# Graph attention layers re-blocked to 4 target tiles, with masks added by DMA, and a scatter spread over 5 stages

## The chip, the cores and the metric

One core of one Trainium2 chip runs the whole program in one launch. The metric is the device time of an execution in microseconds (us); the kernel before takes a median of 7067.14 us over 3 runs (7049.2 to 7069.41). The engines are TensorE (PE, with its weight loads as PEld), VectorE (DVE), ScalarE (ACT), GpSimd (POOL) and SyncE (SP), which only issues DMAs; 16 DMA engines move the data. Engines run on their own and wait for each other by semaphores.

## The reference

A graph of 3125 nodes with 96 features and 103125 directed edges goes through four blocks, each added to its input and normed: three attention layers (GAT), a GIN layer, dot attention, and a layer with edge features. The change touches the GAT layers most:

```
def _gat_layer(x, src, dst, W, a_src, a_dst, b):
    h = (x @ W).reshape(N, H, C)                       # H = 4 heads, C = 24
    alpha_s = jnp.einsum('nhc,hc->nh', h, a_src)
    alpha_d = jnp.einsum('nhc,hc->nh', h, a_dst)
    e = jax.nn.leaky_relu(alpha_s[src] + alpha_d[dst], NEG_SLOPE)
    m = jax.ops.segment_max(e, dst, num_segments=N)
    ex = jnp.exp(e - m[dst])
    den = jax.ops.segment_sum(ex, dst, num_segments=N)
    alpha = ex / (den[dst] + 1e-16)
    out = jax.ops.segment_sum(h[src] * alpha[:, :, None], dst, num_segments=N)
    return out.reshape(N, H * C) + b
for l in range(W.shape[0]):                            # 3 layers
    x = jax.nn.relu(_gat_layer(x, src, dst, W[l], att_src[l], att_dst[l], bias[l]))
```

The last layer of the network sums `relu(x[src] + edge_attr @ We + be)` over the edges of a target. For it the edges' 32 features are scattered in DRAM into an order by source and target tile; that scatter is independent of everything else until the last layer.

## The kernel before, in words

The graph is held dense: nodes are padded to 3200, 25 tiles of 128. `begin` counts the edges of each pair of nodes into a DRAM table by accumulating indirect DMAs, and `make_tables` (L581) turns the counts into `log_counts`, a 3200 x 3200 float table of log counts with a very low value where there is no edge. Attention over edges is then a dense softmax over source nodes with `log_counts` added to the logits.

`gat_attend` (L751) is one GAT layer. Targets go in 5 blocks of 5 tiles (`BT`, `NB`). For a block j, a chunk c of source tiles (9, 8 and 8) and a head h there is a run, 12 runs to a block, 60 to a layer; a unit is one source tile of a run, 100 units to a block. With s and d the source and target terms, `src_row` holds 0.8 s for all sources in every partition. The steps are:

- `maximum` (L885, VectorE): the largest of `near` (half a row of `log_counts`, loaded by SP) plus `src_row`, for a target tile, a head and a half; 40 to a block. The maxima of the next block are spread over the runs of the present one. `columns` (L896) makes the per-target bias `dst_bias` of them.
- `add_bias` (L971, ScalarE): `logit = mask + dst_bias`, where `mask` is a piece of `log_counts` in SBUF, loaded once for four heads. In the last block three of five tiles have it on VectorE instead (L906).
- `finish_logit` (L916, VectorE): `logit = max(src_row, least) + logit`, for each target tile and run, one run ahead of its use; `logit` has 2 buffers.
- TensorE turns each unit's 5 tiles of 128 x 128 into `psE` (L1042, 2 buffers), ScalarE takes the exp of 640 columns into `prob` (L1000), with 0.2 s as its per-source bias, and TensorE multiplies it with the values `hx` (L1029). The values of two source tiles run at once in two groups of 32 columns of the array; heads take the others. A unit's values follow its transposes by `LAG` = 3 units.
- At a block's end ScalarE copies `psO` out, TensorE turns it back, and VectorE sums two parts, divides by the denominator and adds the bias (`output`, L927, 7 chained steps).

The order on every engine is the order in the text of its block; each engine waits at the instruction whose semaphore is not there yet, and all that is queued behind it waits too. SP's loads are sorted by the unit at which their buffer comes free. GpSimd does nothing in a layer but `edge_scatter` (L692), which takes the edges in 62 groups of 13 columns, a third of them in each layer (`LAYER_GROUPS`); each group is two loads, two copies and 13 indirect DMAs of 128 rows of 136 bytes, in 3 stage buffers. `dot_attend` and `make_tables` leave GpSimd idle.

## Time and profile before

| What | us |
|---|---|
| Median of 3 runs | 7067.14 |
| Lowest and highest | 7049.2, 7069.41 |
| The profiled execution | 7061.88 |
| Its span in the trace | 7060.0 |
| Table of logs (`make_tables`) | about 1756 to 1996 |
| First GAT layer, then a projection | about 2003 to 2869, to 2909 |
| Dot attention | about 4960 to 5560 |

Times in the trace count from the start of the span. A group of instructions has a line, an engine, an operation, its output and inputs, their shapes, a count, a busy time and a mean. "Idle before" is the time that the engine stood before them, and behind the arrow is what ended it. PEclk is the clock that TensorE was granted, as a share of 2.4 GHz. Matmuls overlap, and records of VectorE and ScalarE overlap a little, so the cost of one in a row of several is read from start to start. A float32 matmul is two instructions. In the table of stretches a row is start:end, the length, then busy us and instructions of PE, PEld, DVE, ACT and POOL, the granted clock, the busy share of the 16 DMA engines and GB/s.

### The profile page before, as it was taken

Reading aid. Unit: us, or ns where it says so; the run is one execution under the profiler, and the core shown is the slowest. Engines: PE = TensorE matmul, PEld = TensorE weight load, DVE = VectorE, ACT = ScalarE, POOL = GpSimd, SP = SyncE. Lnnn points to the kernel's source line nnn. Section 1 sums busy time; section 2 is a strip of 40 time slices with the busy share of each in tenths; the row PEclk is TensorE's granted clock in tenths of the full one; section 3 lists DMA queues with packets and bytes.
Section 4 is the critical chain, followed back from the end, with each engine's and each line's share of the span. In section 5 each row is a group of like instructions: output and inputs, shape, how many; then the busy total and the mean of one; then the engine's idle time right before and its main releaser. Section 6 shows DMA issues by size and latency. Waiting matters only on the chain. (4 is left out here: it accounts for less than half of the span.)

```text
span 7060.0 us, 64068 instructions
## 1 busy us (share of the span) xinstructions
PE 3859.8 (55%) x22802; PEld 2278.1 (32%) x22802; DVE 4197.0 (59%) x4408; ACT 2725.0 (39%) x3720; POOL 3458.3 (49%) x2713
## 2 busy tenths in 40 slices
PE   2111111110528889488895788877888555445544
PEld 1111011110524445244453444544333233223332
DVE  1434443332789998699986999965899612112113
ACT  1000000000428888288883788840666311111111
POOL 0888878887058830488402884000000155555552
PEclk6555555555769999799997899988888656666566
DMA  9222222222953432233322333233212111111112
GB/s 314 12 7 18 21 15 7 0 0 14 342 203 116 131 108 73 89 112 119 115 78 84 120 117 106 95 121 125 84 66 75 33 39 42 42 39 40 42 40 25
DMA packets 363334, 570.34 MB, mean 81 GB/s; under 512 B 168173, under 2 KB 246027, under 8 KB 358926
## 3 DMA queue, kind: packets, MB, share of 16 engines
q1 hardware_dynamic: 185086, 495.29, 20.9%
q0 software_dynamic: 174720, 69.73, 9.6%
q8 instruction: 187, 3.06, 0.2%
q10 hardware_dynamic: 3216, 1.23, 0.1%
q14 instruction: 125, 1.02, 0.0%
HBM read 451.64 MB, written 114.40 MB: 80 GB/s over the span
## 5 line engine op out<-in xcount | busy, mean ns | idle before, releaser
L313 POOL DMA_INDIRECT counts<-plcell_add,plcell_slot x806 | 1308.8, 1624 | 439.8 <-issue 236.0
L1522 POOL DMA_INDIRECT emxg<-xtab,emsrc x832 | 803.5, 966 | 571.0 <-DVE emsrc L1564 313.5
L396 DVE TENSOR_REDUCE plnlow<-plsame 128x13 f32<-128x1664 bf16 x62 | 117.0, 1888 | 1039.4 <-DMA counts<-plcell_add,plcell_slot 1039.4
L329 PE MATMUL plrows<-ident,plcell 128*128 128x128 f32 x806 | 185.9, 421 | 952.3 <-DVE plsame L388 951.7
L644 ACT ACT_TABLE_LOAD x1 | 1.3, 1283 | 1713.8 <-PE mtps L632 1713.8
L1607 PE MATMUL emps_m<-emwe,emfeatT 128*128 128x384 f32 x416 | 280.0, 768 | 680.5 <-ACT emfeatT L1546 360.6
L1513 POOL IOTA emlocal_id<- 128x128 f32 x1 | 0.2, 237 | 1260.0 <-POOLq L1052 1260.0
L1574 DVE TENSOR_TENSOR emsame<-emlocal_id,emrow 128x512 f32<-128x512 f32 x208 | 144.4, 694 | 695.5 <-DMA plbase_row<-slot_base 488.1
L1546 ACT ACTIVATE emfeatT<-emps_f 128x128 f32<-128x128 f32 x208 | 57.6, 277 | 1198.6 <-remote 746.3
L329 PEld LDWEIGHTS plrows<-ident,plcell 128*128 128x128 f32 x806 | 161.4, 224 | 985.4 <-DVE plsame L388 984.6
L1042 PE MATMUL ga0psE<-ident,ga0logit 128*128 128x128 f32 x2500 | 354.7, 286 | 196.6 <-DVE ga0logit L925 172.3
L1042 PE MATMUL ga2psE<-ident,ga2logit 128*128 128x128 f32 x2500 | 358.0, 287 | 182.8 <-DVE ga2logit L925 165.7
L1042 PE MATMUL ga1psE<-ident,ga1logit 128*128 128x128 f32 x2500 | 354.4, 286 | 187.1 <-DVE ga1logit L925 164.3
L743 POOL DMA_INDIRECT sorted_edges<-ga0sstage,ga0sslot x273 | 385.8, 1413 | 82.8 <-issue 76.8
L1000 ACT ACTIVATE ga2prob<-ga2psE,ga2src_fifth 128x640 f32<-128x640 f32 x500 | 378.5, 793 | 106.6 <-PE ga2psE L1042 101.3
L1000 ACT ACTIVATE ga1prob<-ga1psE,ga1src_fifth 128x640 f32<-128x640 f32 x500 | 377.9, 793 | 105.0 <-PE ga1psE L1042 102.2
L1000 ACT ACTIVATE ga0prob<-ga0psE,ga0src_fifth 128x640 f32<-128x640 f32 x500 | 378.3, 792 | 103.3 <-PE ga0psE L1042 96.7
L743 POOL DMA_INDIRECT sorted_edges<-ga1sstage,ga1sslot x273 | 376.4, 1379 | 82.8 <-issue 76.8
L925 DVE SCALAR_TENSOR_TENSOR ga2logit<-src_row,ga2least,ga2logit 128x1024 f32<-128x1024 f32 (+1 forms) x300 | 396.1, 1341 | 34.1 <-ACT ga2logit L980 31.3
L925 DVE SCALAR_TENSOR_TENSOR ga1logit<-src_row,ga1least,ga1logit 128x1024 f32<-128x1024 f32 (+1 forms) x300 | 396.6, 1343 | 33.1 <-ACT ga1logit L980 32.0
L925 DVE SCALAR_TENSOR_TENSOR ga0logit<-src_row,ga0least,ga0logit 128x1024 f32<-128x1024 f32 (+1 forms) x300 | 397.7, 1346 | 31.2 <-ACT ga0logit L980 28.0
L1616 PEld LDWEIGHTS emps_a<-emmsg,emsame 128*128 128x128 f32 x1664 | 338.2, 272 | 196.7 <-issue 196.1
(320 smaller groups left out, 9525.9 us busy)
## 6 DMA issues: line engine op xcount, KB each, us to landing
counts<-plzeros SPq DMA_DIRECT2D x32, 1250.0 KB
mthalf<-counts SPq DMA_DIRECT2D x50, 800.0 KB, 10.1
log_counts<-mtlogs SPq DMA_DIRECT2D x25, 1600.0 KB
ga0near<-log_counts SPq DMA_DIRECT2D x50, 800.0 KB
ga1near<-log_counts SPq DMA_DIRECT2D x50, 800.0 KB
ga2near<-log_counts SPq DMA_DIRECT2D x50, 800.0 KB
ginhalf<-counts SPq DMA_DIRECT2D x50, 800.0 KB, 7.3
dotlogs<-log_counts SPq DMA_DIRECT2D x25, 1600.0 KB, 6.7
```

The source lines that it names most:

```text
L313: nc.gpsimd.indirect_dma_start(counts[t % 2][:, :], bass.IndirectOffsetOnAxis(ap=cell_slot[:, g % 2, j:j + 1], axis=0), cell_add[:, g % 2, ...
L329: last = nc.tensor.transpose(rows[:, j * P:(j + 1) * P], cell[:, g * G + j:g * G + j + 1].to_broadcast([P, P]), ident[:])
L396: step(nc.vector.reduce_sum(nlow[:], same[:], axis=AX.X))
L743: nc.gpsimd.indirect_dma_start(edges["sorted"][:, :], bass.IndirectOffsetOnAxis(ap=slot[:, t:t + 1], axis=0), stage[:, k, t - i * G, :], N ...
L925: nc.vector.scalar_tensor_tensor(part, src_row[:, h, first:first + width], least[:, j * BT + q, h:h + 1], part, ALU.max, ALU.add).then_inc ...
L1000: nc.scalar.activation(prob[:, u % P_BUFS, :], psE[:, u % 2, 0:BW], ACT.Exp, bias=src_fifth[:, tile(r, t), h:h + 1]).then_inc(exp_ready, 1)
L1042: last = nc.tensor.transpose(psE[:, u % 2, q * P:(q + 1) * P], logit[:, r % 2, q, t * P:(t + 1) * P], ident[:])
L1522: nc.gpsimd.indirect_dma_start(xg[:, h, t, :], None, xtab[:, :], bass.IndirectOffsetOnAxis(ap=src[:, h, t:t + 1], axis=0)).then_inc(gather ...
L1546: nc.scalar.activation(featT[:, v % 2, :], ps_f[:, 0:P], ACT.Copy).then_inc(feat_kept, 1)
L1574: nc.vector.tensor_tensor(same[:, v % 2, :, :], local_id[:].unsqueeze(1).to_broadcast([P, CT, P]), row[:, g % ROWS, lo:lo + CT, ED:ED + 1] ...
L1607: nc.tensor.matmul(ps_m[:, v % 2, 0:CT * D], featT[:, v % 2, :], we[:].rearrange("p t d -> p (t d)"), start=True, stop=True).then_inc(pre_ ...
L1616: last = nc.tensor.matmul(flat_a[:, bass.ds(lo, D)], same[:, w % 2, t, :], msg[:, w % 2, t, :], start=False, stop=(w == CHUNKS - 1 and t = ...
```

## The change

In `gat_attend` the blocks become six of 4 tiles and one of 1 tile (84 runs). Tiles 2 and 3 of a block of four (12 of the 25) are no longer biased by ScalarE and finished by VectorE: VectorE's new `clamp` writes `max(src_row + dst_bias, low_bias)` into `logit`, with `low_bias = dst_bias + least`, and GpSimd issues a DMA that adds `log_counts` to it in SBUF, once per head, with no `mask` buffer. The other 13 tiles keep both steps, and their masks have 4 buffers. Logits are made 2 runs ahead in 3 buffers. The exp takes 512 columns (128 in the last block), `psE` has 3 buffers and `prob` 8. The values of 4 source tiles run at once in the 4 column groups of the array, for one head at a time, and go with the last of their 4 units; the four parts are summed when they are turned back, by small matmuls with `fold` (four identities of 32 on top of each other), so that `output` has 5 steps. Each head's `psO` is kept by ScalarE behind its last run, and `turn_output` follows in run 1 of the next block. The maxima of the next block end in run 9 and its columns stand behind them. The scatter is a generator: GpSimd issues the adds of run r+2, then its share of scatters. Its 62 groups are split 3 to `make_tables`, 16 to each layer and 11 to `dot_attend`, and it has 2 stage buffers.

```diff
-LAYER_GROUPS = ((0, 21), (21, 42), (42, 62))
+TABLE_GROUPS = (0, 3)
+LAYER_GROUPS = ((3, 19), (19, 35), (35, 51))
+DOT_GROUPS = (51, 62)
@@ edge_scatter
-    STAGES = 3
+    STAGES = 2
+                yield t
@@ gat_attend
+        BLOCK_TILES = (4, 4, 4, 4, 4, 4, 1)
-        P_BUFS = 5
-        M_BUFS = 6
+        FOUR = P // VW
+        ADDED = (2, 3)
+        BIAS_AT = (1, 5)
+        P_BUFS = 8
+        M_BUFS = 4
+        E_BUFS = 3
+        AHEAD = 2
+        L_BUFS = AHEAD + 1
+        MAX_RUNS = RUNS - AHEAD
+        steps_done = lambda r: scatter_steps * (r + 1) // len(runs)
@@ GpSimd
-                scatter(pool)
+                def add_masks(r):
+                    for i, q in enumerate(added_tiles(j)):
+                        row = (block_first[j] + q) * P
+                        pool.wait_ge(clamped, add_count[r] + i + 1)
+                        pool.dma_start(logit[:, r % L_BUFS, q, 0:width], log_counts[row:row + P, first:first + width], accum_op=ALU.add).then_inc(mask_added[r % L_BUFS], 16)
+                for r in range(len(runs)):
+                    if r + AHEAD < len(runs):
+                        add_masks(r + AHEAD)
+                    while done < steps_done(r):
+                        next(scattering)
+                        done += 1
@@ VectorE
+                def clamp(r, q):
+                    if r >= L_BUFS:
+                        dve.wait_ge(turned, run_end(r - L_BUFS))
+                    nc.vector.tensor_scalar(logit[:, r % L_BUFS, q, 0:width], src_row[:, h, first:first + width], dst_bias[:, j % 2, q, h:h + 1],
+                                            low_bias[:, j % 2, q, h:h + 1], ALU.add, ALU.max).then_inc(clamped, 1)
+                    if ahead is not None:
+                        for q in added_tiles(ahead):
+                            clamp(r + AHEAD, q)
+                    if run == MAX_RUNS - 1 and j + 1 < BLOCKS:
+                        columns(j + 1)
@@ ScalarE
+                        for at, q in zip(BIAS_AT, kept_tiles(runs[r + AHEAD][0])):
+                            if t == at:
+                                add_bias(r + AHEAD, q)
@@ TensorE
-                    if t % 2 == 0 and t + 1 < RUN_TILES[c]:
+                    if t % FOUR != FOUR - 1 and t + 1 < RUN_TILES[c]:
                         return
+                    for w in range(v - t % FOUR, v + 1):
+                        s = units[w][1]
+                        row = (s % FOUR) * VW
+                        last = nc.tensor.matmul(psO[row:row + VW, h, 0:width], hx[:, tile(r, s), h, :], prob[:, w % P_BUFS, 0:width],
+                            wait(pe, mask_added[r % L_BUFS], 16 * adds_in_buffer(r))
+                    for q in range(BLOCK_TILES[j]):
+                        for h in range(HEADS):
+                            last = nc.tensor.matmul(psT[:, q, h, :], o_sb[:, h, q * P:(q + 1) * P], fold[:], start=True, stop=True)
@@ make_tables and dot_attend
+        scatter, _ = edge_scatter(nc, ctx, a, edges, "mts", *TABLE_GROUPS)
+        scatter, _ = edge_scatter(nc, ctx, a, edges, "dots", *DOT_GROUPS)
```

## Rows read from the trace of the kernel before

**Rows 1.** The page: span, and busy time of each engine.

```profile
span 7060.0 us, 64068 instructions
...
PE 3859.8 (55%) x22802; PEld 2278.1 (32%) x22802; DVE 4197.0 (59%) x4408; ACT 2725.0 (39%) x3720; POOL 3458.3 (49%) x2713
```

**Rows 2.** The table of stretches (columns as told above).

```profile
1756.00:1996.00 240.00, 123.54 (x625) 116.05 (x625) 172.50 (x51) 97.33 (x126) 0.00 (x0) 0.69 0.96 335
...
2003.00:2088.00 85.00, 0.00 (x0) 0.00 (x0) 75.48 (x87) 0.83 (x1) 69.28 (x52) 0.50 0.53 173
...
2088.00:2239.00 151.00, 122.97 (x816) 71.30 (x817) 149.69 (x143) 131.42 (x153) 127.33 (x103) 0.92 0.36 118
...
2239.00:2394.00 155.00, 130.87 (x880) 73.89 (x879) 149.00 (x147) 132.38 (x156) 131.35 (x103) 0.96 0.36 116
...
2544.00:2694.00 150.00, 126.48 (x853) 71.02 (x851) 141.35 (x145) 129.46 (x154) 7.42 (x6) 0.97 0.32 111
...
2694.00:2869.00 175.00, 161.89 (x1152) 93.42 (x1152) 131.86 (x141) 128.66 (x162) 0.00 (x0) 0.99 0.14 45
...
4960.00:5560.00 600.00, 494.56 (x3961) 203.21 (x3962) 562.89 (x522) 399.85 (x624) 0.00 (x0) 0.85 0.19 64
```

**Rows 3.** Groups by form, 2090 to 2700 (busy us, mean ns).

```profile
L925 DVE SCALAR_TENSOR_TENSOR ga0logit<-src_row,ga0least,ga0logit 128x1024 f32<-128x1024 f32 x152 | 196.5, 1310 | 4.7 <-ACT ga0logit L980 4.0 <-issue 0.5
...
L980 ACT ACTIVATE ga0logit<-ga0mask,ga0dst_bias 128x1024 f32<-128x1024 f32 x153 | 175.2, 1145 | 14.2 <-DMA ga0mask<-log_counts 12.5 <-PE ga0psE L1042 1.7
...
L925 DVE SCALAR_TENSOR_TENSOR ga0logit<-src_row,ga0least,ga0logit 128x1152 f32<-128x1152 f32 x80 | 113.8, 1438 | 14.4 <-ACT ga0logit L980 11.9 <-issue 2.5
...
L980 ACT ACTIVATE ga0logit<-ga0mask,ga0dst_bias 128x1152 f32<-128x1152 f32 x78 | 97.8, 1258 | 3.0 <-DVE ga0col L903 1.8 <-DVE ga0dst_bias L904 1.2
```

**Rows 4.** VectorE in order of time, block 0 (start us, us, line, operation).

```profile
2139.11 1.27 DVE L925 SCALAR_TENSOR_TENSOR ga0logit<-src_row,ga0least,ga0logit 128x1024 f32<-128x1024 f32 x1
...
2140.31 1.86 DVE L893 CUSTOM_DVE_ANT_0 ga0unused<-ga0near,src_row 128x1600 bf16<-128x1600 f32 x1
...
2142.10 1.27 DVE L925 SCALAR_TENSOR_TENSOR ga0logit<-src_row,ga0least,ga0logit 128x1024 f32<-128x1024 f32 x1
```

**Rows 5.** All engines in order of time, last block of the layer.

```profile
2789.28 1.14 ACT L980 ACTIVATE ga0logit<-ga0mask,ga0dst_bias 128x1024 f32<-128x1024 f32 x1
...
2790.22 0.77 PE L1042 MATMUL ga0psE<-ident,ga0logit 128*128 128x128 f32 x5
...
2790.31 0.78 ACT L1000 ACTIVATE ga0prob<-ga0psE,ga0src_fifth 128x640 f32<-128x640 f32 x1
...
2793.51 0.75 DVE L914 TENSOR_SCALAR ga0logit<-ga0mask,ga0dst_bias 128x1024 f32<-128x1024 f32 x1
...
2793.85 1.48 ACT L1000 ACTIVATE ga0prob<-ga0psE,ga0src_fifth 128x640 f32<-128x640 f32 x2 [0.35 <-PE ga0psE L1042]
...
2794.17 3.67 DVE L925 SCALAR_TENSOR_TENSOR ga0logit<-src_row,ga0least,ga0logit 128x1024 f32<-128x1024 f32 x3
...
2794.29 1.27 PE L1029 MATMUL ga0psO<-ga0prob,hx 128*32 128x320 f32 x8
...
2795.49 1.31 PE L1042 MATMUL ga0psE<-ident,ga0logit 128*128 128x128 f32 x10
...
2796.73 1.27 PE L1029 MATMUL ga0psO<-ga0prob,hx 128*32 128x320 f32 x8
```

**Rows 6.** TensorE in order of time, dot attention: values in four column groups.

```profile
5209.40 1.28 PE L1376 MATMUL dotpsO<-dotwork,hx 128*32 128x320 f32 x16
```

**Rows 7.** ScalarE's groups of the whole span: a 128-column activation from PSUM.

```profile
L1546 ACT ACTIVATE emfeatT<-emps_f 128x128 f32<-128x128 f32 x208 | 57.6, 277 | 1198.6 <-remote 746.3 <-PE emps_f L1603 330.1 <-issue 122.2
```

**Rows 8.** GpSimd's issue of a direct DMA (min/median/max ns, first and last start).

```profile
L724 POOL DMA_DIRECT2D ga0sfeat<-in_edge_attr_dram x21: 541/590/596, 2006.0 to 2475.4; - x21
```

**Rows 9.** GpSimd's scatters, 2390 to 2540, grouped.

```profile
L743 POOL DMA_INDIRECT sorted_edges<-ga0sstage,ga0sslot x80 | 109.2, 1365 | 24.2 <-issue 22.6 <-POOL ga0sstage L740 1.7
```

**Rows 10.** Finishing steps, 2560 to 2690, where GpSimd is idle.

```profile
L925 DVE SCALAR_TENSOR_TENSOR ga0logit<-src_row,ga0least,ga0logit 128x1024 f32<-128x1024 f32 x27 | 34.2, 1279 | 1.3 <-ACT ga0logit L980 1.3
```

More of the change, by code:

```diff
@@ L600, in make_tables, with _ @@
         pieces = [(j, k) for j in range(NB) for k in range(NB)]
+        scatter, _ = edge_scatter(nc, ctx, a, edges, "mts", *TABLE_GROUPS)
         with nc.Block() as block:
+            @block.gpsimd
+            def _(pool):
+                for _ in scatter(pool):
+                    pass
             @block.sync
@@ L706, in edge_scatter, with steps @@
     scattered = [sem(f"scattered{k}") for k in range(STAGES)]
-    def run(pool):
+    def steps(pool):
         pool.dma_start(slot[:], edges["slot"][:, first * G:last * G]).then_inc(tables_loaded, 16)
@@ L772, in gat_attend @@
         sem = lambda n: nc.alloc_semaphore(tag + n)
+        BLOCK_TILES = (4, 4, 4, 4, 4, 4, 1)
+        BLOCKS = len(BLOCK_TILES)
+        block_first = [sum(BLOCK_TILES[:j]) for j in range(BLOCKS)]
+        MOST = max(BLOCK_TILES)
+        DW = MOST * P
         RUN_TILES = (9, 8, 8)
@@ new lines, in gat_attend @@
+                    g = block_first[j] + q
+                    free = (g - 1) * MAX_PER + HEADS * f + HEADS if g else 0
+                    before = max_run[free - 1] if g else -1
+                    when = first_unit[before] if before >= 0 else -1 + (8 * g + 4 * f) / 100
+                    loads.append((when, 0, ("near", g, f, free)))
+        for n, (j, c, q) in enumerate(mask_uses):
+            if n < M_BUFS:
+                loads.append((-1 + (n + 9) / 100, 1, ("mask", j, c, q, 0)))
+            else:
+                oj, oc, oq = mask_uses[n - M_BUFS]
+                r = oj * RUNS + oc * HEADS + HEADS - 1
+                i = kept_tiles(oj).index(oq)
+                loads.append((first_unit[max(r - AHEAD, 0)] + BIAS_AT[i], 1, ("mask", j, c, q, act_count[r] + i + 1)))
@@ L904, in columns @@
[L904 to L914 removed]
+                    nt = BLOCK_TILES[j]
@@ L927, in output @@
+                    part = logit[:, r % L_BUFS, q, 0:width]
+                    nc.vector.scalar_tensor_tensor(part, src_row[:, h, first:first + width], least[:, block_first[j] + q, h:h + 1], part, ALU.max, ALU.add).then_inc(logit_ready, 1)
                 def output(j):
+                    nt = BLOCK_TILES[j]
                     dve.wait_ge(o_turned, j + 1)
                     step = Chain(dve, out_steps, j * OUT)
-                    yb = y[:, j * BT:(j + 1) * BT, :]
-                    for e in range(2):
-                        for k in range(2):
-                            part = psO[:, k, :, :].rearrange("p f c -> p (f c)")[:, 0:BW].rearrange("p (q h e c) -> p q h e c", h=2, e=2, c=VW)[:, :, :, e, 0:VC]
-                            total = o_sum[:, :, 2 * k:2 * k + 2, :]
-                            last = nc.vector.tensor_tensor(total, total, part, ALU.add) if e else nc.vector.tensor_copy(total, part)
-                        step(last)
@@ new lines, in output @@
+                    step(nc.vector.tensor_scalar(rden[:, 0:nt, :], psT[:, 0:nt, :, DH], 1e-16, None, ALU.add))
+                    step(nc.vector.reciprocal(rden[:, 0:nt, :], rden[:, 0:nt, :]))
+                    step(nc.vector.tensor_tensor(yb.rearrange("p q (h c) -> p q h c", h=HEADS), psT[:, 0:nt, :, 0:DH],
+                                                 rden[:, 0:nt, :].unsqueeze(3).to_broadcast([P, nt, HEADS, DH]), ALU.mult))
+                    step(nc.vector.tensor_tensor(yb, yb, bias[:].unsqueeze(1).to_broadcast([P, nt, D]), ALU.add))
@@ L942, in output @@
                     step(nc.vector.tensor_scalar(yb, yb, 0.0, None, ALU.max))
                     assert step.n == OUT
-                for n in range(MAXIMA):
-                    maximum(0, n)
+                for n in range(max_end(0)):
+                    maximum(n)
                 columns(0)
-                for q in range(BT):
-                    finish_logit(0, q)
+                for r in range(AHEAD):
+                    for q in added_tiles(0):
+                        clamp(r, q)
+                    for q in kept_tiles(0):
+                        finish_logit(r, q)
@@ L962, in _ @@
                             output(j - 1)
-                    if run == RUNS - 2 and j + 1 < NB:
+                    assert next_max == until
+                    if run == MAX_RUNS - 1 and j + 1 < BLOCKS:
                         columns(j + 1)
-                output(NB - 1)
+                output(BLOCKS - 1)
             @block.scalar
@@ L1340, in dot_attend, with _ @@
         flat = lambda n: psS[:, n % S_BUFS, :, :].rearrange("p a c -> p (a c)")[:, 0:BW]
+        scatter, _ = edge_scatter(nc, ctx, a, edges, "dots", *DOT_GROUPS)
         with nc.Block() as block:
+            @block.gpsimd
+            def _(pool):
+                for _ in scatter(pool):
+                    pass
             @block.sync
```

261 lines of the change are left out of this document (123 added, 138 removed).

## The prediction

> **What bounds the kernel now.** I read the page first [rows 1]: no engine is busy over 60% of the span, so the bound is found by stage. The table of stretches of the first attention layer gives it [rows 2]. The layer lasts from 2003 to 2869, 866 us, and the three layers are alike. For 85 us only VectorE works: the 40 maxima of the first block. Then come four stretches of 150 to 155 us, a block of 5 target tiles each (three have rows), with VectorE 141 to 150 us busy, TensorE 123 to 131, ScalarE 129 to 132: VectorE sets the pace. The last 175 us have no maxima; there TensorE is the fullest (162) and the run period is set by it. The projection that follows is unchanged. GpSimd's scatters end before 2544, long before the layer does. The chain of waits covers only the last norm and says nothing here, so the argument goes by stretches, forms and spacing. In the forms [rows 3] and the order of time [rows 4] I take starts, not durations, because VectorE's records overlap: a finishing step of 1024 columns costs 1.20 us (2139.11 to 2140.31), a maximum with its read 1.79 (to 2142.10). The 1152 form is 0.13 longer [rows 3], so a finishing step is 1.24 on average over chunks of 9, 8 and 8 tiles. Check: 60 x 1.24 + 40 x 1.79 = 146, and some 5 for output and columns, 151 against the 150 to 155 of the blocks.
>
> **The change part by part, one layer.**
> *Masking.* 12 of 25 target tiles take a clamp (tensor_scalar on src_row) and an accumulating DMA in place of ScalarE's bias and VectorE's finishing step. 144 tile-runs change. The nearest row of the clamp is the L914 tensor_scalar, 0.75 long and 0.66 before its successor [rows 5]; with the wider form 0.68. VectorE gives back 144 x (1.24 - 0.68) = 81 us, and 36 bias steps of the last block, 25 us.
> *Period of a run in the 4-tile blocks.* An iteration with maxima holds 2 clamps, 2 finishing steps and 3.2 maxima: 1.37 + 2.49 + 5.73 = 9.6 us. For ScalarE, one exp of a pair of 640 columns costs 0.69 (1.48 less 0.78) and at the slope of its 1024 and 1152 forms 0.11 less for 512 [rows 3]: 0.59; a bias 1.03 (2789.28 to 2790.31) to 1.14 [rows 5]. With 8.33 units, and two biases at 1.07: 4.9 + 2.1 = 7.0. For TensorE, two units now take 2.44 (2794.29 to 2796.73) [rows 5]: transposes at 0.108 (5 in 0.77, 10 in 1.31), so 1.08 for ten, some 1.07 of values (the record's 1.27 less a last 0.2 of depth) and 0.3 between. Values of 4 column groups at once are shown by the dot layer: 16 instructions (2 halves, 4 groups, two passes) of 320 columns in 1.28 us [rows 6], as long as the 8 of 2 groups [rows 5]. So a group of 4 tiles of 512 columns costs 1.07 / 2 x 512 / 320 = 0.85 and 0.3 between: 8.33 x 4 x 0.108 + 2.33 x 1.15 = 6.3. Where VectorE has slack, then, ScalarE paces at 7.0; the last stretch, where TensorE paces, still has it busy only 162 of 175 us [rows 2], so for the coupling I put a tenth on top: 7.8. If the 4 groups ran as two pairs, TensorE would need 8.3.
> *A new stall.* All maxima of the next block now end in run 9 of 12, and its columns behind them. The bias of the next block's first run stands in ScalarE's queue at unit 1 of run 10, ahead of run 10's remaining exps, and VectorE reaches the columns only when it has prepared run 11. So ScalarE and behind it TensorE stand for about one iteration, and then VectorE, whose runs 10 and 11 hold only 3.9 us each, waits for two runs at the pace of ScalarE: 15 us in place of 8. A block is 10 x 9.6 + 15 + 3.5 (output, columns) = 114 us; five are 571.
> *Ends.* First maxima: 32 in place of 40 at 1.9, so 85 becomes 69 to the columns, and 9 for preparing two runs instead of one. Block 5, with 8 maxima only, goes by ScalarE: 12 x 7.8 = 94. Block 6 is one tile in 100 units: an exp of 128 columns lasts 0.28 [rows 7], and with one bias a run 3.4 to 4: 43 us, a cost that five equal blocks didn't have. Its tail is 4. Sum 69 + 9 + 571 + 94 + 43 + 4 = 790 against 866: 76 less a layer, 228 for three.
> *The accumulating DMA.* GpSimd issues two a run. No row shows one of this size. Issue: a direct DMA of 127 rows takes 0.59 [rows 8], an indirect one 1.37 [rows 9]; two are 1.2 to 2.7 us a run. A run also issues 2.5 scatters, at 1.9 us each with their copies (80 in 150 us) [rows 9]: 4.7. GpSimd has 6 to 7.4 us of work in 9.6 and is covered. Landing: TensorE wants run r+2 some 6 us after its clamps at the earliest, and because buffers go round in three, a landing up to some 18 us late delays nobody. Traffic: the engines move 335 GB/s at share 0.96 and 111 at 0.32 [rows 2], 348 when full. Per run the near halves (8 of 0.82 MB a block) take 1.6 us, kept masks 0.8, scatters 0.2 (the share is 0.04 higher with some 80 of them in 150 us, 0.08 us each), and the two added tiles 3.1 if an accumulated byte costs as much as a copied one. That is 5.7 of 9.6; at twice the price 8.8, just under. I take it as hidden. Its floor is the copy (no gain below it), its ceiling is open and is the rival below. The Trainium skill, Collectives: The Full Stack, section "The bandwidth ceiling", puts the price of an add in a DMA at its two source reads, half the rate of a copy; by it the sum stays as it is. No row here shows it.
> *Against the change.* The records show GpSimd and VectorE in each other's way: a finishing step lasts 1.31 us over the blocks that are mostly with scatters, 1.28 in a stretch without [rows 3, 10]. The clamp meets the same queue, and its DMAs are issued from it. The Trainium skill, SBUF — State Buffer, box on "DVE blocks DMA", says that such a two-port step keeps GpSimd from writing descriptors; by it landing is late by at most a step's 0.7 us, which the three buffers cover, and the sum would not move.
> *Scatter in 5 stages.* A layer keeps 16 groups of 21. GpSimd passes its last add at about run 69 and then has 37 scatters, 70 us at 1.9, beside 3 runs, the last block and the tail, also 70: even, so 0, at worst 10 a layer. 39 scatters go into the table stage, whose DMA share is 0.96 [rows 2]; 1.4 MB at 335 GB/s are 4 us, with small writes up to 20; I take 5. 143 go into the dot layer, where VectorE is busy 563 of 600 us. The blocks with scatters are 2 us longer on average than the one without for some 80 of them [rows 2]: 4, up to 30 as its tensor_scalar has two ports' worth of reads. Together 9. Output folded by small matmuls into one accumulation is within the stated ends.
> *Sum.* Against the profiled execution, 7061.9 us (span 7060.0): 7062 - 228 + 9 = 6843; its time lies 5 below the median of 7067, so 6848, told as 6850.
>
> **The rivals.**
> *A. The accumulating DMA is the bound (slower).* With added bytes at k times the copy, a run needs 2.6 + 3.1k us of the DMA engines; from k = 2.25 that passes 9.6. At k = 3 a run is 12.0: 60 runs lose 144 and the 12 of block 5 some 40, 184 a layer, so 6850 + 552 = 7400. It loses to the present kernel from about k = 2.5, 1.1 us more a run. For it: the stage of counting accumulates in DRAM and only 2 bytes a row. Against it: a rule of two reads. Between k = 2.25 and 2.5 it eats part of the gain.
> *B. Coupling stays loose (faster, less).* Waits among clamp, DMA, bias and exp bring the 72 four-tile runs to 10.6 us and the last block to 60: 60 x 1.0 + 12 x 2.8 + 17 = 111 a layer, less the boundary waits already in the sum (35), is 76: the gain is gone, 7078. Half of this is likelier, 6965. For it: in the last stretch no engine is full, TensorE at 162 of 175 [rows 2]. Against it: three buffers where there were two.
> *C. No stall at the columns (faster, more).* If ScalarE's queue gets past the bias, the two runs cost 8 and not 15: 5 x 7 x 3 = 105 less, 6745.
> *D. The clock.* TensorE is granted 0.92 to 0.98 while busy 123 to 131 of 150 [rows 2]. In block 6 it works under half the time. At the level of 1.2 GHz a one-tile run still needs less than 5 us; it costs 0 to 10 a layer and stays in the range.
>
> **How the numbers follow.** Forecast with its bounds (6790 to 6910) 0.46; C and what lies near it 0.12; B at half its price, or A just beyond its threshold 0.20; B in full, about equal 0.05; A in full 0.17. The range takes the first three and part of the others: 6740 to 7060. A measurement tells a change from none at about 0.3%, 21 us. Faster: 0.46 + 0.12 + 0.20 = 0.78. Same 0.05. Slower 0.17.
>
> **What would show it.** The clamp's group at 0.75 to 0.85 us, 144 a layer; finishing steps down to 156; blocks of 114 us with a VectorE idle of some 7 us, released by ScalarE, before the first finishing step of each; exps of 512 near 0.68; a last block near 43 us; DMA share near 0.8 to 0.9 at 200 GB/s in the blocks, and TensorE never waiting long for a DMA on the logit tiles. If TensorE's waits before the transposes go to the DMA and the share is over 0.95, A is true. If GpSimd ends each layer alone, the scatter tail is it. Wrong would also be a table stage longer by over 20 us or a dot layer by over 30.

## The result, and the profile after

The changed kernel takes 6994 us (median of four, 6974 to 7006) against 7067 for the kernel before: ratio 0.990, interval 0.9875 to 0.9925, 73 us less. The forecast was 6850, 217 less. The time lies in the range, but two thirds of the forecast gain are missing. The profiled execution took 6973.75 us, 88 less than that of before; it is the fastest of the four, 20 below the median, so the traces show 88 of a forecast 219.

The page of the changed kernel, to be read beside [rows 1] (PEclk, DMA and GB/s are the span in 40 slices):

```profile
span 6972.0 us, 62328 instructions
...
PE 3698.9 (53%) x21452; PEld 2183.6 (31%) x21452; DVE 3889.8 (56%) x4318; ACT 2472.8 (35%) x4050; POOL 4020.6 (58%) x3151
...
DMA  9222222222979987398962898752222111111111
...
q0 software_dynamic: 237024, 305.69, 28.3%
```

VectorE has 307 us less to do, ScalarE 252 less, TensorE 161 less, and the span is only 88 shorter. The first question is therefore not what the work cost but where VectorE now stands idle. One stretch from the start of the first layer to the norm behind the third answers it, in both kernels (columns: stretch and its length, busy time and instructions of PE, PEld, DVE, ACT, POOL, then granted clock, DMA share, GB/s). Before:

```profile
2003.20:4697.00 2693.80, 2081.68 (x13912) 1186.57 (x13912) 2392.05 (x2492) 1990.52 (x2394) 1343.75 (x1060) 0.91 0.31 103
```

After:

```profile
2001.00:4598.10 2597.10, 1913.65 (x12562) 1090.16 (x12562) 2079.47 (x2402) 1737.39 (x2724) 1513.13 (x1257) 0.83 0.75 172
```

VectorE's work in the three layers falls by 313 us (104 a layer); the stretch falls by 97 (32 a layer). Its idle time grows from 302 to 518 us. That is where the gain went: of the 216 us more, 41 lie in the blocks before the last of full size and 175 behind that block's columns, where the three layers end; none lie at the front. The other stages did what was forecast: the table stage went from 246.6 to 251.5 us (+5, as told), the dot layer from 634.5 to 642.0 (+7.5, told +4), the last stage +1, the GIN layer +2; some 7 us less at the very start are not of this change.

The first layer by its own stretches, the counterpart of [rows 2], counted from the columns of one block to those of the next: to the first columns; block 0; block 3; block 5 (the last of four tiles); and, from its first run on, block 6 (one tile).

```profile
2001.00:2068.70 67.70, 0.00 (x0) 0.00 (x0) 59.79 (x71) 0.00 (x0) 0.00 (x0) 0.50 0.43 143
2068.70:2180.60 111.90, 80.16 (x520) 45.77 (x520) 105.95 (x117) 77.90 (x111) 75.15 (x61) 0.84 0.92 209
2414.50:2530.80 116.30, 92.48 (x632) 53.55 (x632) 108.95 (x123) 87.17 (x128) 78.72 (x61) 0.90 0.90 206
2646.60:2740.80 94.20, 88.18 (x618) 50.68 (x619) 66.89 (x75) 86.35 (x128) 71.47 (x65) 0.96 0.93 194
2758.80:2825.10 66.30, 56.24 (x341) 29.17 (x337) 14.96 (x16) 40.21 (x114) 27.92 (x27) 0.53 0.03 7
```

The reader is to see three kinds of stretch. In the middle ones VectorE is nearly full (109 of 116.3). At the front (67.7 us) it works alone, and nothing else can. At the end, in blocks 5 and 6, it has 67 and 15 us of work in 94 and 66, and in the 18 us between the two stretches hardly any. An end of one tile costs 66 us here, 77.9 and 75.1 in the other two layers, and VectorE sleeps through it.

Groups by form in the second layer, to be read beside [rows 3]:

```profile
L928 DVE CUSTOM_DVE_ANT_0 ga1unused<-ga1near,src_row 128x1600 bf16<-128x1600 f32 x200 | 366.2, 1831 | 8.9 <-DMA ga1near<-log_counts 6.7
L958 DVE SCALAR_TENSOR_TENSOR ga1logit<-src_row,ga1least,ga1logit 128x1024 f32<-128x1024 f32 x104 | 136.2, 1310 | 62.0 <-ACT ga1logit L1017 43.6 <-issue 18.4
L898 POOL DMA_DIRECT2D ga1logit<-log_counts x144 | 136.1, 1065 | 292.1 <-DVE ga1logit L949 287.0 <-issue 5.0
L958 DVE SCALAR_TENSOR_TENSOR ga1logit<-src_row,ga1least,ga1logit 128x1152 f32<-128x1152 f32 x52 | 73.9, 1425 | 66.5 <-ACT ga1logit L1017 57.8 <-issue 8.7
L949 DVE TENSOR_SCALAR ga1logit<-src_row,ga1dst_bias,ga1low_bias 128x1024 f32<-128x1024 f32 x96 | 73.8, 809 | 0.1
L949 DVE TENSOR_SCALAR ga1logit<-src_row,ga1dst_bias,ga1low_bias 128x1152 f32<-128x1152 f32 x48 | 40.2, 879 | 2.2 <-PE ga1psE L1086 2.0
```

Finishing steps and maxima last what they lasted. The clamp, 144 a layer, takes 0.81 and 0.88 us; the accumulating DMA 1.07 us of GpSimd's time to issue. Of VectorE's idle time before finishing steps, 128 us in this layer, 101 end with ScalarE's bias, L1017.

The waits in block 3 of the first layer:

```profile
PE ga0psE L1086 <- DMA ga0logit<-log_counts: 11.6, 5, 5.0
...
ACT ga0logit L1017 <- DVE ga0low_bias L941: 7.1, 1, 7.1
...
DVE ga0logit L958 <- ACT ga0logit L1017: 6.3, 4, 2.5
```

### The profile page after: what moved, and what is told of

Same layout as the page of the kernel before. It is cut to its first block and busy times, and to the rows that moved or that the text cites. A ratio compares the mean times of both kernels' runs of the same rounds, so it can differ in the third digit from the quotient of the medians.

```text
span 6972.0 us, 62328 instructions
## 1 busy us (share of the span) xinstructions
PE 3698.9 (53%) x21452; PEld 2183.6 (31%) x21452; DVE 3889.8 (56%) x4318; ACT 2472.8 (35%) x4050; POOL 4020.6 (58%) x3151
## 3 DMA queue, kind: packets, MB, share of 16 engines
q0 software_dynamic: 237024, 305.69, 28.3%
q14 instruction: 131, 1.07, 0.0%
## 5 line engine op out<-in xcount | busy, mean ns | idle before, releaser
L1086 PE MATMUL ga0psE<-ident,ga0logit 128*128 128x128 f32 x2500 | 406.9, 303 | 219.1 <-DMA ga0logit<-log_counts 151.4
L1040 ACT ACTIVATE ga1prob<-ga1psE,ga1src_fifth 128x512 f32<-128x512 f32 (+1 forms) x700 | 405.4, 667 | 153.6 <-PE ga1psE L1086 130.5
L1040 ACT ACTIVATE ga2prob<-ga2psE,ga2src_fifth 128x512 f32<-128x512 f32 (+1 forms) x700 | 405.0, 665 | 152.0 <-PE ga2psE L1086 123.6
L1040 ACT ACTIVATE ga0prob<-ga0psE,ga0src_fifth 128x512 f32<-128x512 f32 (+1 forms) x700 | 405.6, 669 | 139.4 <-PE ga0psE L1086 124.9
L1086 PEld LDWEIGHTS ga2psE<-ident,ga2logit 128*128 128x128 f32 x2500 | 293.7, 151 | 448.1 <-issue 265.1
L1086 PEld LDWEIGHTS ga0psE<-ident,ga0logit 128*128 128x128 f32 x2500 | 293.8, 151 | 447.0 <-issue 252.9
L1086 PEld LDWEIGHTS ga1psE<-ident,ga1logit 128*128 128x128 f32 x2500 | 291.3, 150 | 453.0 <-issue 280.2
L1668 PE MATMUL emps_a<-emmsg,emsame 128*128 128x96 f32 x1664 | 387.5, 375 | 22.8 <-DVE emsame L1626 8.5
L1470 ACT ACTIVATE dotwork<-dotpsS 128x640 f32<-128x640 f32 x500 | 313.1, 708 | 205.9 <-PE dotpsS L1418 204.5
L1502 DVE TENSOR_TENSOR dotwork<-dotwork,dotcnt 128x1280 f32<-128x1280 f32 x250 | 374.8, 1499 | 8.6
```

The source lines that it names most:

```text
L1040: nc.scalar.activation(prob[:, u % P_BUFS, 0:width], psE[:, u % E_BUFS, 0:width], ACT.Exp, bias=src_fifth[:, tile(r, t), h:h + 1]).then_in ...
L1086: last = nc.tensor.transpose(psE[:, u % E_BUFS, q * P:(q + 1) * P], logit[:, r % L_BUFS, q, t * P:(t + 1) * P], ident[:])
L1470: nc.scalar.activation(work[:, t % W_BUFS, 2 * g:2 * g + 2, f * HW:(f + 1) * HW], psS[:, n % S_BUFS, :, 0:HW], ACT.Exp).then_inc(exp_ready, 1)
L1502: nc.vector.tensor_tensor(w, w, cnt[:, t % C_BUFS, cols].unsqueeze(1).to_broadcast([P, HEADS, HW]), ALU.mult).then_inc(prob_ready, 1)
L1668: last = nc.tensor.matmul(flat_a[:, bass.ds(lo, D)], same[:, w % 2, t, :], msg[:, w % 2, t, :], start=False, stop=(w == CHUNKS - 1 and t = ...
```

## The experiments

Every run is compared with the kernel before on the same chip (medians 7050 and 7063 there, and 6726 for the two runs that are marked). For the layers I give beside the time the length of the stretch shown above, first near load of layer 0 to the norm behind layer 2, from each profiled execution (before 2693.8, changed kernel 2597.1), because it leaves out what other stages do from run to run: on the first two of these chips they took, from that norm to the end, 2351 to 2402 us, though no edit here touches them. A stretch is one execution.

**Scatters done before the last block.**

```diff
-        steps_done = lambda r: scatter_steps * (r + 1) // len(runs)
+        steps_done = lambda r: scatter_steps * min(r + 1, 6 * RUNS) // (6 * RUNS)
```

> The same scatters, spread over the runs of the first six blocks (2.9 a run in place of 2.5), so that GpSimd is done before the one-tile block. Theory G (in the changed kernel the last block takes 66 to 78 us because TensorE and ScalarE stand while GpSimd issues its last scatters; once GpSimd is done, a run takes 4.0 us): the block falls to 12 x 4.0 and some 6 for the fold of block 5, 54 us, so 12 to 24 less a layer, 50 for three: 6940. Theory S (the gaps come from the short runs themselves, the chain bias, finish, transpose, exp): the block keeps 66 to 78 us and the time stays at 6990 within 15.

Measured: 6932 us, ratio 0.982 (0.979 to 0.984); stretch 2560.0. The one-tile block takes 57.3, 57.2 and 56.9 us in the three layers where it took 66.3, 77.9 and 75.1, 48 less in all. The stretch is only 37 shorter, because the blocks of four in layer 2 became 10 us longer together. In the second layer of the changed kernel, the stretch of that block up to shortly after GpSimd's last scatter, and the stretch behind it:

```profile
3628.30:3662.70 34.40, 16.69 (x96) 9.70 (x88) 5.93 (x8) 8.54 (x23) 25.23 (x27) 0.55 0.06 13
3662.70:3706.20 43.50, 41.00 (x249) 19.67 (x249) 8.99 (x7) 31.56 (x91) 0.00 (x0) 0.50 0.00 1
```

and the whole block in this kernel, where GpSimd is silent:

```profile
3613.20:3670.40 57.20, 55.25 (x341) 28.82 (x337) 14.93 (x15) 39.72 (x114) 0.00 (x0) 0.54 0.00 1
```

With GpSimd issuing, 23 instructions of ScalarE are done in 34 us; without, 91 in 43. The changed kernel in order of time shows how (start, length, engine; in brackets the idle time before):

```profile
3651.53 0.48 PE L1086 MATMUL ga1psE<-ident,ga1logit 128*128 128x128 f32 x1
...
3651.92 0.37 ACT L1040 ACTIVATE ga1prob<-ga1psE,ga1src_fifth 128x128 f32<-128x128 f32 x1
...
3652.50 0.69 PE L1086 MATMUL ga1psE<-ident,ga1logit 128*128 128x128 f32 x2
...
3659.85 0.96 POOL L750 DMA_INDIRECT sorted_edges<-ga1sstage,ga1sslot  x1 [0.30 <-issue]
...
3662.76 0.37 ACT L1040 ACTIVATE ga1prob<-ga1psE,ga1src_fifth 128x128 f32<-128x128 f32 x1 [10.46 <-remote]
3663.18 0.18 PEld L1086 LDWEIGHTS ga1psE<-ident,ga1logit 128*128 128x128 f32 x1 [10.39 <-ACT ga1prob L1040]
3663.18 0.48 PE L1086 MATMUL ga1psE<-ident,ga1logit 128*128 128x128 f32 x1 [9.99 <-ACT ga1prob L1040]
```

ScalarE stands for 10.46 us, and the view names no instruction that released it ("remote"). TensorE stands behind it, and both go on 2 us after the last scatter is issued.

The semaphore events in the same trace say what ScalarE lacked. Its next exp waits for `turned`, which TensorE raises with each transpose. The transpose of that exp starts at 3651.53, and the next rise of `turned` is recorded at 3662.74, 11.2 us later; the exp starts 0.02 us behind it. In the edited kernel, with GpSimd silent, the rise comes 0.49 us after the start of the transpose. I summed these late rises, where ScalarE stood for one: they cost 9.3, 20.7 and 18.9 us in the one-tile blocks of the changed kernel, some 4 us in each block 5, and nothing in the blocks before it. In the edited kernel they cost nothing in the one-tile blocks, which are 8.9, 20.7 and 18.2 us shorter. So the whole standstill is TensorE's signal that comes late. Whether the transpose itself is held up or only its signal, and by what of GpSimd's scatters (their issue or their writes), the records do not tell: the ends of matmuls are modelled.

Theory G holds: the block falls to 57, and S, which kept 66 to 78, falls. Against the forecast of 43 + 4, some 10 us a layer are left even so.

**The added tiles copied instead of accumulated.**

```diff
-... log_counts[row:row + P, first:first + width], accum_op=ALU.add).then_inc(...)
+... log_counts[row:row + P, first:first + width]).then_inc(...)
```

> The 144 DMAs a layer onto logit copy and don't accumulate: the same bytes from the same queue, and what is left out is the clamped term of target tiles 2 and 3 of each block, so their attention is not the layer's. Theory D (the accumulating DMAs, twice as dear per packet in the records, hold the four-tile blocks at 116.5 us in place of the 114 forecast): blocks fall to 112 or less, 15 to 25 less a layer, about 6930. Rival (VectorE sets the pace, the DMA is hidden in the three buffers): the DMA share falls from over 0.9 to near 0.65, the blocks stay within 1 us and the time within 15 us of 6990.

Measured: 6953 us, ratio 0.986 (0.984 to 0.988); stretch 2576.3. The same block and its bytes:

```profile
2402.20:2518.50 116.30, 93.73 (x632) 54.36 (x632) 108.24 (x123) 87.17 (x128) 73.25 (x61) 0.90 0.60 206
```

The block is as long as before, 116.3 us at the same 206 GB/s, while the share falls from 0.90 to 0.60. The four middle blocks of the three layers average 117 us in both kernels. TensorE's waits before the transposes that end with a landing are 11.6 us in this block of the changed kernel and 6.7 with the copy, and the 5 us less shorten nothing. So the accumulation costs the DMA engines 0.30 x 116.3 = 35 us a block, and costs the block nothing: D is wrong, the DMA is hidden. The 35 us are for 24 DMAs of 0.55 MB on average, 1.45 us each; at the 348 GB/s of [rows 2] a copy of that size takes 1.57, so an accumulated byte costs 1.9 times a copied one (an estimate from these rows). The line of the queue on the two pages agrees, for the same bytes 28.3% with accumulation and here

```profile
q0 software_dynamic: 237024, 305.69, 19.0%
```

which is about 1.5 us more for each of the 432 DMAs. The Trainium skill (Collectives: The Full Stack, section "The bandwidth ceiling") says that an add in a DMA needs two source reads where a copy needs one; it tells this of ReduceScatter. The 1.9 here agrees with it.

The stretch is 21 us shorter all the same. Block 0 went from 112, 111 and 115 us to 106 in the three layers, which is 20 of the 21. The first transposes start 10.2 us behind the columns with the accumulating DMA and 7 to 8 with the copy, so about 3 of the 6 us are the first landing; the rest is not separated. The last block varies as in the changed kernel (76.6, 67.5, 76.4).

**Three tiles of four accumulated.**

```diff
-        ADDED = (2, 3)
-        BIAS_AT = (1, 5)
+        ADDED = (1, 2, 3)
+        BIAS_AT = (1,)
```

> From the changed kernel: three tiles of each block masked by accumulating DMA. By work, VectorE has 12 x 0.6 less a block (101 us). The DMA engines are busy 105 us of 116.5 with two; the plain copy of the same bytes had them busy 70 of 117, so 24 accumulating DMAs cost 70 and 36 cost 105, with 25 to 30 of other traffic: 130 to 135 us. Theory A (beyond a share near 1 the DMA sets the block): blocks of 133, block 5 near 115, a layer longer by 5 x 16.5 + 20 = 103, so 6990 + 310 = 7300. If the DMA never set the pace: blocks of 110 and 6890.

Measured: 7035 us, ratio 0.996 (0.994 to 0.998); stretch 2663.6. A block in the middle:

```profile
2419.50:2539.50 120.00, 98.74 (x648) 57.81 (x645) 103.89 (x123) 76.96 (x117) 87.09 (x73) 0.87 1.06 245
```

VectorE has 5 us less to do than with two added tiles, ScalarE 10, and the block is not shorter: 114 to 120 us. The recorded share is 1.06, the highest of any run; it adds up the times of packets, so it can pass 1. TensorE waits seven times for more than 1.5 us in this block, 19 us in all, and by the records of landings each of these waits ends 0.1 us after an added tile lands. From the last issue of a run's added tiles to their landing it takes 14.9 us (median), where it took 9.3 with two tiles and 5.1 with two plain copies. So rival A of the prediction is real and lies one tile further on. The engines' time, 1.06 x 120 = 127 us, is near the 130 told; wrong was to take 1 for the highest share that the record can show, so blocks are 114 to 120 and not 133.

**One tile of four accumulated.**

```diff
-        ADDED = (2, 3)
-        BIAS_AT = (1, 5)
+        ADDED = (3,)
+        BIAS_AT = (1, 4, 6)
```

> Only tile 3 of each block is masked by DMA, tile 2 goes back to ScalarE's bias and VectorE's finishing step. If VectorE and ScalarE set the pace (rival of D): a run with maxima is longer by a finishing step less a clamp, 1.30 - 0.75 = 0.55, so 50 x 0.55 = 28 a layer and block 5 longer by 12 biases of 1.1, 13: three layers +120, 7110. Theory D (the accumulating DMAs hold the blocks): half their traffic gone gives back 3 us a run before VectorE's 0.55 is paid; the blocks stay at 116 or fall, and the time is 6990 or less.

Measured: 7139 us, ratio 1.012 (1.008 to 1.016), slower than before; stretch 2763.4. Blocks are 129.3 us in place of the 122 forecast:

```profile
2438.50:2567.80 129.30, 98.42 (x632) 56.38 (x632) 114.31 (x122) 99.72 (x140) 61.26 (x49) 0.88 0.61 147
```

and the wait that grew in it:

```profile
DVE ga0logit L958 <- ACT ga0logit L1017: 14.6, 7, 6.0
```

VectorE's work grew by 5.4 us, as told; the other 8 are VectorE waiting for biases, 14.6 us a block where it was 6.3, because ScalarE now has three biases a run. A second cause is mixed in: three kept tiles share the 4 mask buffers that two had, and ScalarE waits 27 us in the first layer for masks to be loaded, for which it does not wait in any other kernel with added tiles. A tile masked by DMA is worth more than its VectorE time in this kernel; how much of that is the mask buffers was not tested. With one tile of four the kernel loses against the one before.

**The one-tile block first.**

```diff
-        BLOCK_TILES = (4, 4, 4, 4, 4, 4, 1)
+        BLOCK_TILES = (1, 4, 4, 4, 4, 4, 4)
```

> The one-tile block comes first. Theory S or G alike (the one-tile block is dear because it stands at the end, where VectorE has no maxima left, and the first maxima stand alone): 8 first maxima in place of 32, 15 us and not 68; a one-tile block beside the 32 maxima of the next takes 32 x 1.85 + 12 x 1.35 and the columns, some 80; five blocks of 116.5; the last of four tiles 94; 9 to prepare and 4 to end: 785 a layer against 827 to 839. So 6990 - 3 x 48 = 6845. If instead the boundary waits or the near loads eat it (a short first block has its 32 maxima behind loads that start late), the gain is under half, 6920 or more.

Measured: 6860 us, ratio 0.973 (0.971 to 0.974); stretch 2486.1. The first layer: first maxima, the one-tile block beside 32 maxima, a full block, the last:

```profile
2002.00:2018.40 16.40, 0.00 (x0) 0.00 (x0) 15.57 (x21) 0.00 (x0) 11.87 (x8) 0.50 0.60 213
2018.40:2095.30 76.90, 43.64 (x256) 20.15 (x256) 74.07 (x81) 39.73 (x99) 35.31 (x24) 0.50 0.36 116
2326.80:2443.40 116.60, 92.15 (x632) 53.31 (x632) 108.99 (x124) 86.86 (x128) 79.09 (x61) 0.90 0.90 206
2690.00:2790.70 100.70, 95.40 (x673) 55.07 (x672) 44.35 (x46) 84.43 (x128) 57.73 (x57) 0.97 0.71 133
```

The same instructions, 62328 of them, in another order: the short block lies where VectorE is busy anyway (74 of 77 us), and the exposed maxima fall from 68 to 16 us. Forecast 6845; a gain of some 120 us over the changed kernel by the ratios, 111 by the stretch, where 144 were told.

**Columns one run earlier.**

```diff
-        MAX_RUNS = RUNS - AHEAD
+        MAX_RUNS = RUNS - AHEAD - 1
```

> From the changed kernel: the maxima of the next block end in run 8 and its columns follow there, one run earlier. Theory C (the wait of ScalarE for the columns, 9.4 us at each boundary, costs VectorE the 6 to 7 us that it stands idle per block): 5 x 6.5 = 33 less a layer, 6990 - 98 = 6892. Rival R (VectorE has only moved its slack: nine runs now hold 3.56 maxima and last 10.4 us, 94; three runs hold none and go by ScalarE's 7.2 to 7.8, 23): a block stays at 117 to 120 and the time at 6990 to 7030, though the wait for the columns is gone from the records.

Measured: 7001 us, ratio 0.991 (0.989 to 0.994); stretch 2639.3, 42 us longer than in the changed kernel, with blocks of 119 to 123 behind the first. In such a block:

```profile
DVE ga0logit L958 <- ACT ga0logit L1017: 9.7, 4, 4.6
```

The wait of ScalarE for the columns, 7.1 us in the changed kernel, is gone from the list, and nothing is won: VectorE now idles 9.7 us for biases. Rival R holds; C, as this edit realizes it, falls. Nine crowded runs and three empty ones cost VectorE more than the wait did. The edit moves the maxima together with the columns, so it takes the run with the columns left where they were, below, to part the two.

**Maxima in every run.**

```diff
-        max_until = lambda j, run: max_first(j) + BLOCK_TILES[j] * MAX_PER * min(run + 1, MAX_RUNS) // MAX_RUNS
...
+        max_points = [(0, max_end(0))] + [(j * RUNS + MAX_RUNS, max_end(j + 1)) for j in range(BLOCKS - 1)]
+
+        def max_until(r):
+            for (t0, n0), (t1, n1) in zip(max_points, max_points[1:]):
+                if r + 1 <= t1:
+                    return n0 + (n1 - n0) * (r + 1 - t0) // (t1 - t0)
+            return max_points[-1][1]
```

This stands on top of the two edits before it (one-tile block first, columns one run earlier). The dots stand for a table, `max_run`, that follows the new order.

> One-tile block first; columns one run earlier; and the maxima no longer stop for the boundary: in the three runs behind the columns VectorE already takes the first maxima of the block after the next, so that each run holds 2.67 of them. If VectorE sets the pace (busy 109 of 116.5 us in a block): a block falls to 110 or 111, six less in six blocks of three layers, 108: 6860 - 108 = 6752. Rival D (the DMA engines, busy 0.90 of 116.5 us = 105, are the next limit): their share passes 0.95, transposes wait for landings, and blocks stay at 114 or more: 6815 and up.

Measured: 6769 us, ratio 0.9585 (0.955 to 0.962); stretch 2396.0. A block and the three layers:

```profile
2419.00:2527.00 108.00, 91.65 (x628) 53.59 (x620) 107.65 (x122) 86.06 (x128) 79.95 (x62) 0.92 0.96 222
...
1995.90:4391.90 2396.00, 1905.29 (x12562) 1094.80 (x12562) 2077.29 (x2403) 1738.46 (x2724) 1592.74 (x1257) 0.86 0.81 187
```

VectorE is busy 107.65 of 108.00 us: it has no wait left in the middle blocks, and the DMA engines are at 0.96 beside it without being the limit. VectorE's work in the stretch is what it was in the changed kernel (2077 against 2079); its idle time fell from 518 to 319 us, and that is the whole gain of 201. This kernel beats both.

**The same, with the columns left where they were.** This run and the next were on another chip, on which the kernel before takes 6726 us, because the last stage is quicker there; ratios are compared, not times.

```diff
-        MAX_RUNS = RUNS - AHEAD - 1
+        MAX_RUNS = RUNS - AHEAD
```

> As the kernel with maxima in every run (6769), but the columns stay behind run 9 of 12, as in the changed kernel. If the maxima behind the columns do all the work and the place of the columns none: VectorE is busy to the end of the block anyway, 6770 within 15. If ScalarE's wait for the columns (7 to 9 us at a boundary) still comes back to VectorE through the biases of the next block's first run: some 3 to 6 us in six blocks of three layers, 6820 to 6870.

Measured: 6443 us, ratio 0.958 (0.957 to 0.960), against 0.9585 with the columns earlier; stretch 2399.8 against 2396.0. In a middle block (108.4 us) ScalarE still waits 7.3 us for the columns, as in the changed kernel, and VectorE is busy 107.7 us all the same. So the place of the columns does none of this step's gain; the even spread of the maxima does all.

**Blocks of 2, 4, 4, 4, 4, 4 and 3 tiles.**

```diff
-        BLOCK_TILES = (1, 4, 4, 4, 4, 4, 4)
+        BLOCK_TILES = (2, 4, 4, 4, 4, 4, 3)
```

> As the kernel with maxima in every run (6769), with blocks of 2, 4, 4, 4, 4, 4 and 3 tiles. The last block goes by TensorE and ScalarE: 12 runs of 7.8 us (94) with four tiles, some 6.4 (77) with three, while VectorE's own work in it is 47 and 40. Total VectorE work is fixed, so a layer is that work less its part in the last block plus the last block: 17 less for the block, 7 more because less of VectorE's work lies in it, and 7 more for one masked tile fewer (12 x 0.6): 3 less a layer, 6760 within 15. Rival (the coupling in short runs is loose, as in the one-tile block): the last block keeps 85 or more and the time is 6790 or above.

Measured: 6449 us, ratio 0.959 (0.957 to 0.960); stretch 2401.8. The edit stands on the kernel with maxima in every run and the columns one run earlier. No difference from the seven blocks that begin with one tile can be told, as the sum of 3 us a layer said.

**Nearly no scatters in layer 1.** On the kernel with the one-tile block first.

```diff
-LAYER_GROUPS = ((3, 19), (19, 35), (35, 51))
+LAYER_GROUPS = ((3, 26), (26, 28), (28, 51))
```

> From the kernel with the one-tile block first (6860): layers 0 and 2 take 23 groups of scatters each, layer 1 only 2. If GpSimd and VectorE stand in each other's way (K): in layer 1 the clamp of 1024 columns lasts 0.75 in place of 0.81 us, the finishing step 1.28 in place of 1.32, and its five full blocks fall by 24 x 0.06 + 24 x 0.04 = 2.4 us each to 114; layers 0 and 2 grow by 1 each a block, or more where GpSimd, with 3.6 scatters a run at 1.9 and two adds at 1.0, needs 8.9 of 9.7 us. Rival: durations and blocks are alike in all three layers within 0.5 us. Total 6845 to 6885 either way.

Measured: 6895 us, ratio 0.976 (0.973 to 0.978); stretch 2523.6. The same block in layer 0 (299 scatters) and in layer 1 (26):

```profile
2331.36:2448.82 117.46, 94.78 (x632) 54.92 (x632) 108.67 (x123) 87.39 (x128) 103.99 (x81) 0.89 0.91 206
...
3178.26:3294.78 116.52, 95.13 (x632) 55.31 (x632) 107.26 (x122) 87.16 (x128) 29.17 (x30) 0.88 0.87 198
```

GpSimd's work falls from 104 to 29 us and VectorE's by 1.4; the block by 1. The finishing step of 1024 columns lasts 1.284 us in layer 1 and 1.299 in layer 0, the clamp 0.808 and 0.827. K is right in sign and half of what was told, and the clamp's 0.81 is its own, not GpSimd's doing. The stretch is nevertheless 37 us longer than with even groups. Of this, 24 lie at the ends of layers 0 and 2, where GpSimd has scatters left that nothing paces: from the last columns to the end 129 us in layer 0 and 127 in layer 2 (115 and 117 with even groups), and 114 in layer 1. The blocks of four in layer 2 are 22 us longer together, 10 of them in one block, and layer 1 gives 11 back. TensorE in order of time at that place in layer 0, and GpSimd's last scatter:

```profile
2796.41 1.11 PE L1086 MATMUL ga0psE<-ident,ga0logit 128*128 128x128 f32 x4 [4.36 <-ACT ga0prob L1040]
```

```profile
2792.79 0.96 POOL L750 DMA_INDIRECT sorted_edges<-ga0sstage,ga0sslot  x1 [0.30 <-issue]
```

It looks like the standstill of the one-tile block, in a block of four tiles, and it ends again 2 to 3 us after the last scatter. Late rises of `turned` cost 6.3 us in this block and 5.2 in that of layer 2, about half of the 14 and 10 us there. For the rest, and for the longer blocks of layer 2, where no rise is late, I have no cause.

## Why the prediction was right or wrong

A layer was told to take 790 us and takes 824, 838 and 836 (from 866). By its steps:

| step | told | measured, layers 0, 1, 2 |
|---|---|---|
| to the first columns | 69 | 68, 69, 68 |
| from the start to the one-tile block | 743 | 758, 760, 761 |
| of this, a block of four tiles in the middle | 114 | 116 to 118 |
| block 5 by ScalarE | 94 | 94 |
| one-tile block with its tail | 47 | 66, 78, 75 |

**The step that failed is the one-tile block.** It was costed at 43 us and a tail of 4 from the length of a 128-column activation and one bias a run [rows 7], and takes 66 to 78. This term is 26 us a layer of the 43 missing, in two parts.

The first part is 9 to 21 us of standing still beside GpSimd's scatters, which the first experiment takes away. The prediction had looked at GpSimd's tail there, for its end only ("even, so 0"). It does end in time; it costs because TensorE's signals reach ScalarE late meanwhile.

The second part is some 10 us that stay. With GpSimd silent a run of eight tiles takes 4.0 us, the upper end of what was told (3.4 to 4), and a run of nine 4.8, above it: 8 x 4.0 + 4 x 4.8 = 51 where 43 were told. In such a run ScalarE waits 0.5 to 0.6 us at a time for transposes, and a single transpose lasts 0.48 us at the granted clock of 0.50 to 0.54. In the kernel before it lasts 0.27, in a stretch at 0.99:

```profile
2788.82 0.27 PE L1042 MATMUL ga0psE<-ident,ga0logit 128*128 128x128 f32 x1
```

So the run was priced by ScalarE's work alone, and TensorE's transposes at the lower level of its clock lie in the chain too. What the clock is worth there was not tested by a run. Block 5's fold, 32 small matmuls in 5.0 us of TensorE with everything behind them, is most of the other 2 us (an estimate by what is left).

**A block of four, 114 against 116.5.** Five times 2.3 is 12 a layer. It lies in VectorE's steps. From start to start, as the prediction measured, a clamp costs 0.73 us (1024) or 0.80 (1152), 0.75 on average over a block's runs, where 0.68 was put from a tensor_scalar on other operands [rows 5]: 24 x 0.07 = 1.7 us a block. A finishing step costs 1.27 where 1.24 was put, 0.7 a block; a maximum costs its 1.79. The remaining 3 to 6 us a layer are not placed.

**The boundary was right as a wait and wrong as a cause.** VectorE does idle 6 to 7 us, released by ScalarE, as told. But rival C, which gave back 105 us if the wait at the columns were gone, is refuted: with the columns earlier the wait is gone and the time is 7001, and with the maxima in every run and the columns left where they were the wait is there and VectorE does not idle for it. The idle time comes from runs without maxima, in which ScalarE's pace holds. It goes when VectorE has maxima in every run, with or without the wait.

**The accumulating DMA was right**: hidden at two tiles of four, at 1.9 times the price of a copy, share 0.90 at 206 GB/s (told 0.8 to 0.9 at 200), issue 1.0 to 1.1 us (told 0.6 to 1.4). Not foreseen were 5 to 8 us in the first block of each layer, of which the landing of the first tiles, which no buffer hides, is about half. Rival A lies one tile further. On the box that the prediction named (Trainium skill, SBUF — State Buffer, "DVE blocks DMA"): in the changed kernel the issue of an add lasted 1.0 us in the median and 1.34 at most, so no add was held up by as much as the 0.7 us that the prediction allowed for it. ScalarE's exps at 0.72 us on average, the table stage and the dot layer came as told, +5 and +7.5. The clock (D) fell to 0.90 in the blocks and to 0.53 in the one-tile block; its 0 to 10 us a layer are not refuted, and most of the second part above may be the clock.

**Rival B had the place right, not the mechanism.** It let the four-tile runs slacken to 10.6 us and the last block to 60, by waits among clamp, DMA, bias and exp. The first hardly happened (116.5 us a block), the last went beyond, by signals that no rival had. Its half price, 6965, is nearest to what came; that is luck. So is that the time fell inside the wide range.

**Two readings were off, without weight in the sum.** GpSimd's scatters in the first layer before end at 2553, not before 2544, and the last 175 us of that layer still hold maxima until 2713; its last block proper takes 130 us.

**What the sum did not ask.** I costed the change stretch by stretch and never set VectorE's total work against the layer. That sum shows at once that taking 104 us of work from a layer cannot shorten the layer by 104 when 68 us of it stand alone at the front and blocks 5 and 6 hold some 12% of it in a fifth of the time.

## What to carry to other kernels

When the bounding engine gets less work, write down its idle time before and after, and where it lies: here 313 us of work went and 216 us of idle time came, 41 at the block boundaries and 175 at the ends of the layers, in the last full block and the short one. A remainder block belongs where the bounding engine has other work, at the front, and prework for the next block should fill every run, not stop for a boundary; those two orders of the same work were worth 0.990 to 0.9585. An accumulating DMA is a cheap way to take an addition off an engine as long as the DMA engines keep up with its double price: here at a share of 0.90 and 0.96, no longer at 1.06.

## What the runs showed of the hardware

- Accumulating DMA from DRAM onto SBUF, 0.55 MB: 1.9 times the engines' time of a copy, 1.0 to 1.1 us of GpSimd's time to issue. Two to a run land 9.3 us after their last issue (5.1 as copies) and hold nothing up, at shares of 0.90 to 0.96. Three to a run land after 14.9 us, at 245 GB/s and a recorded share of 1.06, and TensorE waits for them; issuing one then takes 1.37 us in the median.
- While GpSimd issues indirect DMAs without a pause (0.96 us each, every 1.27 us), the semaphore that TensorE raises with a transpose rises up to 11.2 us after the transpose starts, in place of 0.49, and ScalarE and TensorE stand for up to 10.5 us at a time. This costs 9 to 21 us in a block of very short instructions. Where scatters are paced by the runs, 2.5 to 3.6 to one, no rise is late, though some blocks of layer 2 are up to 4 us longer in the kernel with 2.9 and up to 10 in that with 3.6. Which resource they share was not found.
- Two chips: the stages up to the last agree (the stretch of three layers 2396 and 2400 us for kernels alike but for the columns), while from the first edge rows to the last norm one takes 1455 us and the other 1129.
